# Router products with the router weights held instead of the tokens, and the logits turned back by VectorE, in a one-core attention and mixture-of-experts layer

## The reference

```python
normed = _layernorm(hidden_states, ln_w, ln_b)
xf = normed.reshape(-1, h)
logits = xf @ router_w                       # (4096, 256) @ (256, 8)
top_idx = jnp.argmax(logits, axis=-1)
top_score = jax.nn.sigmoid(jnp.max(logits, axis=-1))
...
w = jnp.where(top_idx == e, top_score, 0.0)[:, None]
xe = xf * w
hmid = jax.nn.silu(xe @ g) * (xe @ u)        # summed over the 8 experts
...
shared = jax.nn.silu(xf @ sh_gate) * (xf @ sh_up) @ sh_down
```

## Time and profile before

| what | us |
|---|---|
| median of 3 runs | 1027.32 (1026.43 to 1033.72) |
| profiled execution, its own time | 1030.09 |
| span of its trace | 1028.4 |
| mean granted TensorE clock in it | 0.987 of full |

### The profile page before, as it was taken

One profiled execution on the slowest core, in us unless ns is written; L12 is line 12 of the kernel. 1 busy time (PEld: TensorE's weight loads), 2 busy tenths in 40 slices (PEclk: granted clock), 3 DMA queues, 4 the chain that ended last, 5 costly groups with the idle time before them and its releaser, 6 DMA issues. The chain is left out here.

```text
span 1028.4 us, 19085 instructions
## 1 busy us (share of the span) xinstructions
PE 989.2 (96%) x6302; PEld 598.5 (58%) x6302; DVE 701.0 (68%) x1733; ACT 475.6 (46%) x685; POOL 363.8 (35%) x482
## 2 busy tenths in 40 slices
PE   7998899999999999999999899999999999999993
PEld 3556344444443444444443466666666999999993
DVE  4887888888888888889874265565565445445442
ACT  2453366766667666667666422221222333333330
POOL 7994232222221222222222123334443243333342
PEclk9999899999999999999999999999999999999997
DMA  7798443434554654534500457222162222222220
GB/s 286 173 243 193 69 63 59 61 60 70 94 94 74 105 78 71 103 57 94 102 11 12 133 172 240 78 84 83 42 206 75 64 75 71 77 76 69 79 80 21
DMA packets 79821, 100.16 MB, mean 97 GB/s; under 512 B 28049, under 2 KB 66449, under 8 KB 76401
## 3 DMA queue, kind: packets, MB, share of 16 engines
q1 hardware_dynamic: 66208, 72.65, 34.1%
q0 software_dynamic: 4944, 13.77, 3.7%
q10 hardware_dynamic: 8576, 12.58, 3.7%
HBM read 65.86 MB, written 32.70 MB: 96 GB/s over the span
## 5 line engine op out<-in xcount | busy, mean ns | idle before, releaser
L1055 ACT ACTIVATE probs<-scores_ps 128x1024 f32<-128x1024 f32 (+3 forms) x384 | 290.5, 809 | 139.9 <-PE scores_ps L981 138.1
L301 DVE TENSOR_REDUCE maxima<-max_ps 128x1 f32<-128x512 f32 (+2 forms) x352 | 232.0, 688 | 38.4 <-PE max_ps L259 20.2
L259 PE MATMUL max_ps<-k_stack,q_stack 96*128 96x512 bf16 (+3 forms) x768 | 221.6, 331 | 2.6 <-DVE maxima L296 1.2
L1146 POOL TENSOR_SCALAR_AFFINE_SELECT probs<-probs 128x512 f32<-128x512 f32 x128 | 81.3, 635 | 323.2 <-ACT probs L1055 323.2
L981 PE MATMUL scores_ps<-q_stack,k_stack 99*128 99x512 bf16 (+3 forms) x768 | 182.9, 327 | 3.0 <-PEq L359 1.6
L1001 PE MATMUL out_ps<-probs,v_ones 128*32 128x512 f32 (+3 forms) x1536 | 163.7, 498 | 2.3 <-POOL probs L1146 1.8
L296 DVE CUSTOM_DVE_ANT_0 masked_out<-max_ps,mask_wide 128x384 bf16<-128x384 f32 (+1 forms) x256 | 151.5, 622 | 19.2 <-PE max_ps L259 16.6
L259 PEld LDWEIGHTS max_ps<-k_stack,q_stack 96*128 96x128 bf16 x768 | 74.6, 97 | 149.6 <-DVE maxima L296 55.7
L1442 ACT ACTIVATE silu<-gate_ps 128x512 f32<-128x512 f32 x71 | 42.4, 597 | 232.1 <-PE gate_ps L1355 135.6
L981 PEld LDWEIGHTS scores_ps<-q_stack,k_stack 99*128 99x128 bf16 x768 | 69.6, 99 | 52.6 <-ACT probs L1055 8.0
L1522 DVE TENSOR_TENSOR hidden_t<-silu,up_ps 128x512 f32<-128x512 f32 x39 | 26.8, 688 | 100.0 <-PE up_ps L1368 100.0
(11 more groups left out here) (169 smaller groups left out, 1297.8 us busy)
## 6 DMA issues: line engine op xcount, KB each, us to landing
k_stack<-k_parts SPq DMA_DIRECT2D x96, 128.0 KB, 4.4
q_stack<-q_parts SPq DMA_DIRECT2D x96, 128.0 KB, 7.2
q_parts<-parts SPq DMA_DIRECT2D x32, 192.0 KB, 3.2
k_parts<-parts SPq DMA_DIRECT2D x32, 192.0 KB, 3.2
rows_in<-expert_rows SPq DMA_DIRECT2D x39, 136.0 KB, 2.1
sums_in<-expert_sums SPq DMA_DIRECT2D x39, 128.0 KB, 2.0
x_t<-in_x_cols SPq DMA_DIRECT2D x8, 512.0 KB, 11.2
heads_rows<-heads_out SPq DMA_DIRECT2D x32, 128.0 KB, 2.1
```

The lines of the kernel that those rows point to most:

```text
L259: last = nc.tensor.matmul(part, self.q_stack[:ROWS, u.slot, h0 + k, t * P:(t + 1) * P], self.k_stack[:ROWS, u.slot, h0 + k, chunk * BLOCK: ...
L301: nc.vector.tensor_reduce(self.maxima[:, u.slot, chunk, h0:h0 + heads, t], self.bank("piece", u.i, n)[:, :heads * keys].rearrange("p (h k) ...
L1055: nc.scalar.activation(probs[:, s % RING, 2 * pair:2 * pair + 2, n0:], scores_ps[:, pair, :, n0:], ACT.Exp).then_inc(exp_done, 1)
L1146: nc.gpsimd.affine_select(out=tile, in_=tile, compare_op=ALU.is_ge, fill=0.0, base=0, pattern=[[0, GROUP], [1, P]], channel_multiplier=-1) ...
```

## The change

`route` holds the router's weights and streams the tokens. The weights are padded from 8 to 32 columns with zeros (`QUAD`), and for each half of the width four matmuls of 128 columns each are made: quarter q takes tokens q to q + 31 of each of the four tiles and writes to partitions q to q + 31. The number of matmuls stays 8. The result has experts on partitions and tokens along the row, so `choose` begins with one more DVE instruction, a transpose of 128 x 128 by blocks of 32 x 32 from PSUM into a new tile `logits`; the next two instructions read this tile instead of PSUM. `VEC_STEPS` grows by the one `link`. POOL clears the padded router tile in unit 0 as the 12th constant (`CONSTS` 15), and SP's load of the router waits for the constants and writes 8 of every 32 columns.

```diff
-    VEC_STEPS = 16
-    CONSTS = 14
+    QUAD = 32
+    VEC_STEPS = 17
+    CONSTS = 15
...
-        self.router = b.sb("router_sb", [P, DC, EXPERTS])
+        self.router = b.sb("router_sb", [P, DC, self.QUAD])
+        self.logits = b.sb("logits", [P, BT, self.QUAD])
...
-        for t in range(BT):
-            for c in range(DC):
-                last = nc.tensor.matmul(self.route_ps[:, t * EXPERTS:(t + 1) * EXPERTS],
-                                        self.xf_t[:, odd, c, t * P:(t + 1) * P], self.router[:, c],
+        for c in range(DC):
+            tokens = self.xf_t[:, odd, c].rearrange("p (t n) -> p t n", t=BT)
+            for q in range(0, P, self.QUAD):
+                last = nc.tensor.matmul(self.route_ps[q:q + self.QUAD, :P].rearrange("p (t n) -> p t n", t=BT),
+                                        self.router[:, c], tokens[:, :, q:q + self.QUAD],
                                         start=(c == 0), stop=(c == DC - 1))
...
-        logits = self.route_ps[:, :BT * EXPERTS].rearrange("p (t e) -> p t e", e=EXPERTS)
+        self.link(dve, i, nc.vector.transpose(self.logits[:].rearrange("p t q -> p (t q)"), self.route_ps[:, :P]))
+        logits = self.logits[:, :, :EXPERTS]
...
-        pool.wait_ge(self.const_step, 11)
+        nc.gpsimd.memset(self.router[:], 0.0).then_inc(self.const_step, 1)
+        pool.wait_ge(self.const_step, 12)
...
-        sp.dma_start(self.router[:], io["router_w"].rearrange("(c p) n -> p c n", p=P)).then_inc(self.small_in, 16)
+        sp.wait_ge(self.const_step, self.CONSTS)
+        sp.dma_start(self.router[:, :, :EXPERTS], io["router_w"].rearrange("(c p) n -> p c n", p=P)).then_inc(self.small_in, 16)
```

## The result

| | before | changed |
|---|---|---|
| median of 11 runs, us | 1032.38 (1026.43 to 1034.19) | 1022.18 (1019.41 to 1024.65) |
| ratio, 95% interval | | 0.9909 (0.9892 to 0.9926) |
| profiled execution / span, us | 1030.09 / 1028.4 | 1023.55 / 1021.7 |

The ratio makes 9.4 us of 1032.4 (7.6 to 11.1), where 8.4 were forecast. It is the ratio that has to be compared: the three runs of before that the forecast started from had their median in the lower part of what its later runs cover.

A forecast was written before the change was run, and what follows sets the result against it. The prediction took PE's queue to bound the kernel in `feed`. Six blocks at 6.3 us, block 7 at 0.8 and block 0 at 1.35 made 8.4 us, from median 1027.32 to 1018.9 us, range 1015.8 to 1023.5.

The forecast's parts named there:

- PE's queue is the bound, so the route's time counts in full: In `feed`, PE's queue sets the end, so time PE saves is gained: 1.05 us per block, 6.3 us over six.
- 0.57 us for the packed route, 0.09 us for going in: PE's cost of the changed route per block, priced from `times_v` in `attend`: 0.66 us in place of 1.71 us.
- The drains that speak against the change: Switching between whole-array and packed matmuls drains PE: 0.09 + 0.15 us a block, 1.7 us over seven.
- The transpose at 0.29 us, hidden: DVE's new transpose between route and choice takes 0.29 us and delays nothing in six blocks, with 0.5 us of room.
- The dear transpose: Rival: DVE's transpose takes up to 1.23 us and costs 3.6 us in all, giving 1022.5 us; chance 0.10.
- Block 7, 0.8 us: The last route in `feed` gains only 0.8 us, with small waits at `down(6, 3)` and for `chosen_bf`.
- Block 0, 1.35 us: The route in `attend` shares the form of the `times_v` ahead, so everything to the end of `attend` moves 1.35 us earlier.
- What costs nothing: POOL's clearing in unit 0, SP's wait for constants in unit 4 and the router's load add no time.
- The quarters in single file: Rival: the route's quarters don't run beside each other, 1.95 us against 1.71, giving 1029 to 1042 us; chance 0.05.
- The term left out of the sum: PE's slow clock at the turn from `attend` to `feed` might shift, making the gain 1.7 us larger or smaller.
- The base: The starting time for the whole kernel: median 1027.32 us, with the profiled execution of 1030.09 us 2.8 us above it.

The follow-up runs named there:

- the unpacked kernel: The changed kernel with all route matmuls written to partitions 0 to 31 one after another, transpose on 32 partitions; median 1032.5 us, ratio 1.0008 to before.

## Why the prediction was right, and where it was off

- *PE's queue is the bound, so the route's time counts in full.* Right: the six distances give 6.07 us.
- *0.57 us for the packed route, 0.09 us for going in*, borrowed from `times_v`. Measured 0.575 (0.584 in the last) and 0.094 us. The saving per block was 1.01, not 1.05 us: 0.02 of the difference is rounding, and 0.02 are lost in `turn_heads` (0.93 instead of 0.91 us). 6.1 instead of 6.3 us.
- *The drains that speak against the change.* They are there and cost what the rows of `attend` said.
- *The transpose at 0.29 us, hidden.* 0.32 us, hidden with 0.45 us of room where 0.5 was reckoned. The dear transpose is refuted by its row; what it would have done is seen in the kernel with three of them.
- *Block 7, 0.8 us.* 0.72 us.
- *Block 0, 1.35 us.* The tail is shorter by just that.
- *What costs nothing.* Nothing in the traces waits for the router's load or the constants. The start up to 564 us is 0.81 us longer, well within the 2.6 us by which it varies over the traces.
- *The quarters in single file.* The rival's price, 1.95 us against 1.71 before, is what the unpacked kernel measured (1.96). The changed kernel does not do it, in either loop order.
- *The term left out of the sum*, the clock. The prediction looked for it at the turn to `feed` and let it go either way by 1.7 us. It went both ways. At the turn it took 1.05 us back, in the execution profiled and in each of the six traces with the route packed in `attend`, against an execution of the lower group. In `attend`, where the profile of before showed a full clock and the prediction had no reason to look, the change ended a fall that most executions of before have; it costs them 2.2 us there and goes together with 1.05 us at the turn, and the two groups of times are some 4 us apart. The step that was mis-sized is this one. The work itself was 8.1 us against 8.4.
- *How much of it was luck.* The 8.4 us of the sum lie near the 9.4 us measured because these lie between two kinds of execution. The same change gains 7.5 us over the one and 10.4 over the other, and of the eleven runs of before behind the ratio five were of the lower group and six of the upper. The terms on PE and DVE came out by their mechanism; that the whole did so well came also from clock terms of either sign that the sum didn't hold.
- *The base.* One profiled execution, and three runs of which one (1033.72) already lay 6 us above the others, were read as one kernel with a little noise. The absolute forecast of 1018.9 us was 3.3 us under the measured median for that.

What stays open is why the old form is followed by the fall in some executions and not in others, which property of the form matters, and why the turn has 3.4 us at 1.2 GHz behind tails of 9.7 us (three traces) and 6.8 us behind both the tails of 8.4 us (six) and of 12.0 us (four). The runs show that both happen, and with which form of the route, not what the chip counts.

## What to carry to other kernels

This fp32 product with 8 columns on one side cost PE 0.11 us a pass whichever operand was held; it got cheap when the small operand was held in four quarters of 32 columns and the products ran beside each other, and then the way into and out of that form, 0.24 us here, has to be paid by what is saved. The price of a form can be taken from another place of the same trace, by starts against starts and at two sizes: here 0.57 us was forecast and 0.575 measured. Where the times of one kernel fall into two groups, take a trace of each before forecasting a change: a change that removes the cause of the upper group gains more than the work it removes.

## What the runs showed of the hardware

- Passes issued quarter by quarter overlap as well as passes issued in rotation (0.595 against 0.575 us for 16), so here the issue order didn't have to follow the packing.
- Sixteen passes of 8 columns in 1.8 us in `attend` were followed from about their end on, in four of five traces, by 6.8 us at 1.2 GHz while PE went on working; sixteen of 128 columns in the same time by none, in two traces of two. PE counted as busy in both. What was held differed too (128 columns against 32). The same sixteen passes of 8 columns in `feed` were never followed by such a stretch.
- A tail 1.28 us shorter (8.41 us against 9.69) was mostly taken back by 3.4 more microseconds at 1.2 GHz at the turn: 0.25 us of it were left at block 1's route, and the times are the same (1019.4 to 1024.7 us against 1020.3 to 1023.8).
